# Another order of steps on every engine in a batch-pipelined transformer kernel

## The reference

```
L0: x  = LN(x  + MHA(x, ctx; 16 heads of 16, causal, length mask))    attention 0
    x  = LN(x  + MHA(x, ctx; 16 heads of 16, length mask))            attention 1
    x  = LN(x  + live * (fc2(relu(fc1(x)))))
L1: h  = x + Wo * GQA(rms(x), rms(ctx); 16 heads of 64, 4 kv heads, rope, additive mask)   attention 2
    x  = h + Wdown * (silu(Wgate rms(h)) * (Wup rms(h)))              width 1024
L2: x  = x + Wo * MHA(LN(x), LN(ctx); 16 heads of 16)                 attention 3
L3: x  = LN(x + Wo * MHA(x, ctx; 16 heads, scores * f(mask), clipped to +-50))             attention 4
```

## Time and profile before

| what | value |
|---|---|
| median of three runs | 4441.46 us |
| the profiled execution's own time | 4448.31 us |
| its span | 4446.5 us |
| granted TensorE clock, mean | 0.99 of full speed |
| busy: TensorE matmul / weight load | 92% / 78% of the span |
| busy: VectorE / ScalarE / GpSimd | 66% / 61% / 28% of the span |
| first store issued / 61st store issued | 246.99 us / 4283.08 us |

### The profile page before, as it was taken

One profiled execution on the slowest core, in us unless ns is written; L12 is line 12 of the kernel. 1 busy time (PEld: TensorE's weight loads), 2 busy tenths in 40 slices (PEclk: granted clock), 3 DMA queues, 4 the chain that ended last, 5 costly groups with the idle time before them and its releaser, 6 DMA issues.

```text
span 4446.5 us, 116614 instructions
## 1 busy us (share of the span) xinstructions
PE 4086.8 (92%) x45024; PEld 3473.5 (78%) x45024; DVE 2928.1 (66%) x7395; ACT 2694.5 (61%) x8513; POOL 1233.9 (28%) x2247
## 2 busy tenths in 40 slices
PE   4899999999999999999999999999999999999996
PEld 3778778787787787787787887787787877877875
DVE  2576676676666666766766766766766766766664
ACT  2566666656656656656656666666666666566563
POOL 0232322322322322323323323323223223223221
...
DMA packets 47341, 52.92 MB, mean 12 GB/s; under 512 B 5328, under 2 KB 46288, under 8 KB 46416
## 3 DMA queue, kind: packets, MB, share of 16 engines
...
## 4 chain that ended last, share of the span: by engine, by line
PE 42%; DVE 40%; issue 10%; POOL 5%; ACT 2%; DVEq 0%; DMA 0%; POOLq 0%; ACTq 0%
PE gen_ps L481 25%; PE gen_ps L473 9%; DVE negmax L957 4%; DVE masked L944 4%; POOL rstd L779 4%; DVE masked L951 4%; PE gen_ps L598 3%; DVE st L919 2%; DVE xs L929 2%; DVE zn L914 2%; ACT prob L724 2%; PE gen_ps L587 2%; PE scores_ps L556 2%; DVE negmax L946 2%; PE scores_ps L563 1%
## 5 line engine op out<-in xcount | busy, mean ns | idle before, releaser
L481 PE MATMUL gen_ps<-actT,w_sb 128*128 128x128 f32 x11264 | 1394.5, 277 | 3.4 <-ACT actT L694 3.3
L481 PEld LDWEIGHTS gen_ps<-actT,w_sb 128*128 128x128 f32 x11264 | 1325.8, 193 | 23.0 <-ACT actT L694 6.2
L724 ACT ACTIVATE prob<-scores_ps,negmax 128x128 f32<-128x128 f32 x3072 | 859.8, 406 | 330.6 <-DVE negmax L957 330.6
L779 POOL TENSOR_TENSOR rstd<-ve,consts 128x1 f32<-128x1 f32 x448 | 282.9, 631 | 1525.0 <-DVE ve L921 1000.0
L473 PE MATMUL gen_ps<-consts,prob 128*128 128x128 f32 x4096 | 591.0, 279 | 65.1 <-ACT prob L724 63.1
L694 ACT ACTIVATE probT<-gen_ps 128x512 f32<-128x512 f32 x1024 | 585.8, 638 | 59.7 <-PE gen_ps L473 59.7
L473 PEld LDWEIGHTS gen_ps<-consts,prob 128*128 128x128 f32 x4096 | 467.8, 142 | 184.9 <-ACT prob L724 147.2
L957 DVE TENSOR_REDUCE negmax<-scores_ps 128x4 f32<-128x512 f32 x768 | 492.0, 682 | 82.7 <-PE scores_ps L563 82.2
L481 PE MATMUL gen_ps<-w_sb,actT 128*128 128x256 f32 x2048 | 532.3, 383 | 2.7 <-ACT actT L694 1.9
L481 PE MATMUL gen_ps<-w_sb,wide 128*128 128x256 f32 x2048 | 467.9, 381 | 1.2 <-issue 1.2
L694 ACT ACTIVATE actT<-gen_ps 128x256 f32<-128x256 f32 (+1 forms) x576 | 276.5, 480 | 301.4 <-PE gen_ps L473 294.0
...
## 6 DMA issues: line engine op xcount, KB each, us to landing
ctx_rms<-x_dram SPq DMA_DIRECT2D x64, 128.0 KB, 2.2
ctx<-ctx_dram SPq DMA_DIRECT2D x64, 128.0 KB, 2.2
mask<-mask_dram SPq DMA_DIRECT2D x128, 64.0 KB, 2.0
out_dram<-res SPq DMA_DIRECT2D x64, 128.0 KB, 1.7
...
```

The lines of the kernel that those rows point to most:

```text
L481: last = nc.tensor.matmul(ps, lhsT(c), rhs(c), start=(c == 0), stop=(c == chunks - 1))
L724: ins = nc.scalar.activation(prob[:, N % 4, k, :], scores_ps[:, u, k * S:(k + 1) * S], ACT.Exp, bias=negmax[:, N % 4, k:k + 1])
L779: nc.gpsimd.tensor_tensor(dst, src, const("expo")[:, 0:width], ALU.pow)\
```

## The change

`PERIOD` goes from 66.01 to 67.32 and all times in `LIFE` are others. No step is added or removed, and no wait, buffer or instruction is altered; what changes is the order in which each of the four engines meets the steps. The core of the diff:

```diff
-PERIOD = 66.01
+PERIOD = 67.32
...
-    ("xT", 0, 0, {"PE": 0.00, "ACT": 2.67, "DVE": 14.33}),
-    ("queries", 0, 0, {"PE": 16.81, "DVE": 24.76}),
-    ("keys", 0, 0, {"PE": 17.38, "ACT": 22.00}),
...
+    ("xT", 0, 0, {"PE": 2.23, "ACT": 0.00, "DVE": 15.62}),
+    ("queries", 0, 0, {"PE": 8.34, "DVE": 18.60}),
+    ("keys", 0, 0, {"PE": 12.59, "ACT": 20.84}),
...
-    ("attended", 0, 0, {"PE": 49.73, "DVE": 52.29, "POOL": 44.45}),
-    ("q2", 2, 1, {"PE": 118.91, "DVE": 122.20, "POOL": 112.04}),
+    ("attended", 0, 0, {"PE": 60.47, "DVE": 70.60, "POOL": 66.81}),
+    ("q2", 2, 1, {"PE": 125.81, "DVE": 134.69, "POOL": 123.09}),
...
-    ("norm", 4, 0, {"DVE": 250.95}),
+    ("norm", 4, 0, {"DVE": 270.05}),
```

More of the change, by code:

```diff
@@ new lines @@
+    ("xT", 0, 0, {"PE": 2.23, "ACT": 0.00, "DVE": 15.62}),
+    ("queries", 0, 0, {"PE": 8.34, "DVE": 18.60}),
+    ("keys", 0, 0, {"PE": 12.59, "ACT": 20.84}),
+    ("first_row", 0, 0, {"PE": 28.83, "DVE": 35.23}),
+    ("scores", 0, 0, {"PE": 35.17}),
+    ("soft", 0, 0, {"ACT": 39.93, "DVE": 52.57}),
+    ("soft", 0, 1, {"ACT": 48.63, "DVE": 52.58}),
+    ("soft", 0, 2, {"ACT": 50.15, "DVE": 54.63}),
+    ("soft", 0, 3, {"ACT": 50.61, "DVE": 54.91}),
+    ("turn", 0, 0, {"PE": 50.81, "ACT": 51.92}),
@@ new lines @@
+    ("turn", 0, 1, {"PE": 50.83, "ACT": 53.93}),
+    ("turn", 0, 2, {"PE": 51.20, "ACT": 54.22}),
+    ("turn", 0, 3, {"PE": 52.20, "ACT": 54.53}),
+    ("values", 0, 0, {"PE": 59.02, "ACT": 59.88}),
+    ("attended", 0, 0, {"PE": 60.47, "DVE": 70.60, "POOL": 66.81}),
+    ("stats", 0, 0, {"DVE": 72.35, "POOL": 68.27}),
+    ("ctx_norms", 0, 0, {"DVE": 72.01, "POOL": 76.98}),
+    ("tr", 1, 0, {"PE": 72.31, "ACT": 72.06}),
+    ("norm", 0, 0, {"DVE": 76.79, "POOL": 73.71}),
+    ("queries", 1, 0, {"PE": 73.76, "DVE": 82.99}),
@@ new lines @@
+    ("keys", 1, 0, {"PE": 74.92, "ACT": 74.53}),
+    ("first_row", 1, 0, {"PE": 76.06, "DVE": 89.90}),
+    ("scores", 1, 0, {"PE": 83.79}),
+    ("soft", 1, 0, {"ACT": 89.90, "DVE": 90.57}),
+    ("soft", 1, 1, {"ACT": 91.02, "DVE": 92.87}),
+    ("turn", 1, 0, {"PE": 91.61, "ACT": 98.08}),
+    ("turn", 1, 1, {"PE": 93.97, "ACT": 98.66}),
+    ("soft", 1, 2, {"ACT": 97.90, "DVE": 95.09}),
+    ("turn", 1, 2, {"PE": 95.14, "ACT": 101.36}),
+    ("turn", 1, 3, {"PE": 96.98, "ACT": 102.02}),
+    ("values", 1, 0, {"PE": 97.61, "ACT": 102.27}),
@@ new lines @@
+    ("soft", 1, 3, {"ACT": 97.97, "DVE": 100.17}),
+    ("attended", 1, 0, {"PE": 99.83, "DVE": 110.20, "POOL": 102.65}),
+    ("x2T", 1, 0, {"PE": 102.91, "ACT": 105.93}),
+    ("h", 1, 0, {"PE": 105.25, "ACT": 109.16}),
+    ("z", 1, 0, {"PE": 106.66, "DVE": 123.12, "POOL": 109.83}),
+    ("stats", 1, 0, {"DVE": 116.20, "POOL": 107.35}),
+    ("mean_square", 2, 0, {"DVE": 124.66, "POOL": 111.85}),
+    ("norm_x3", 1, 0, {"ACT": 116.79, "DVE": 123.14}),
+    ("norm", 1, 0, {"DVE": 119.39}),
+    ("tr", 2, 0, {"PE": 120.38, "ACT": 125.10}),
@@ new lines @@
+    ("q2", 2, 1, {"PE": 125.81, "DVE": 134.69, "POOL": 123.09}),
+    ("q2", 2, 0, {"PE": 124.24, "DVE": 132.22}),
+    ("rms_norm", 2, 0, {"DVE": 125.81}),
+    ("kv2", 2, 0, {"PE": 127.74, "DVE": 137.21, "POOL": 131.56}),
+    ("scores", 2, 0, {"PE": 134.16}),
+    ("soft", 2, 0, {"ACT": 139.86, "DVE": 145.37}),
+    ("soft", 2, 1, {"ACT": 140.13, "DVE": 145.76}),
+    ("prob_norm", 2, 0, {"DVE": 154.41, "POOL": 145.41}),
+    ("soft", 2, 2, {"ACT": 149.54, "DVE": 147.97}),
+    ("turn", 2, 0, {"PE": 150.47, "ACT": 155.38}),
@@ new lines @@
+    ("soft", 2, 3, {"ACT": 151.13, "DVE": 150.69}),
+    ("turn", 2, 1, {"PE": 151.36, "ACT": 156.49}),
+    ("prob_norm", 2, 1, {"DVE": 154.58, "POOL": 156.79}),
+    ("turn", 2, 2, {"PE": 156.86, "ACT": 157.62}),
+    ("prob_norm", 2, 2, {"DVE": 157.55, "POOL": 156.97}),
+    ("turn", 2, 3, {"PE": 157.99, "ACT": 158.37}),
+    ("out2", 2, 0, {"PE": 158.68, "ACT": 159.54}),
+    ("out2", 2, 1, {"PE": 158.87, "ACT": 165.03}),
+    ("prob_norm", 2, 3, {"DVE": 161.13, "POOL": 163.02}),
+    ("o2", 2, 0, {"PE": 161.83, "ACT": 166.51, "DVE": 167.60}),
@@ new lines @@
+    ("nT", 3, 0, {"PE": 164.69, "ACT": 169.52}),
+    ("gate", 3, 0, {"PE": 166.58, "ACT": 170.54, "DVE": 181.48}),
+    ("mean_square", 3, 0, {"DVE": 169.45, "POOL": 166.60}),
+    ("up", 3, 0, {"PE": 167.92, "DVE": 186.98}),
+    ("rms_norm", 3, 0, {"DVE": 170.47}),
+    ("gate", 3, 1, {"PE": 171.47, "ACT": 175.80, "DVE": 187.54}),
+    ("up", 3, 1, {"PE": 173.98, "DVE": 189.66}),
+    ("down", 3, 0, {"PE": 182.99, "DVE": 192.29, "POOL": 181.59}),
+    ("tr", 3, 0, {"PE": 187.15, "ACT": 190.39}),
@@ new lines @@
+    ("queries", 3, 0, {"PE": 190.14, "DVE": 196.18}),
+    ("keys", 3, 0, {"PE": 190.95, "ACT": 193.00}),
+    ("scores", 3, 0, {"PE": 192.62}),
+    ("norm_x4", 3, 0, {"DVE": 194.47}),
+    ("soft", 3, 0, {"ACT": 194.50, "DVE": 199.82}),
+    ("soft", 3, 1, {"ACT": 195.52, "DVE": 199.99}),
+    ("turn", 3, 0, {"PE": 195.83, "ACT": 198.14}),
+    ("soft", 3, 2, {"ACT": 196.61, "DVE": 200.33}),
+    ("soft", 3, 3, {"ACT": 198.01, "DVE": 202.35}),
+    ("turn", 3, 1, {"PE": 198.18, "ACT": 199.36}),
@@ new lines @@
+    ("turn", 3, 2, {"PE": 198.55, "ACT": 200.92}),
+    ("turn", 3, 3, {"PE": 201.24, "ACT": 201.53}),
+    ("values", 3, 0, {"PE": 204.21, "ACT": 203.44}),
+    ("attended", 3, 0, {"PE": 207.70, "DVE": 213.90}),
+    ("zT", 3, 0, {"PE": 209.69, "ACT": 212.54}),
+    ("o", 3, 0, {"PE": 213.84, "DVE": 224.80, "POOL": 213.93}),
+    ("tr", 4, 0, {"PE": 215.51, "ACT": 221.83}),
+    ("queries", 4, 0, {"PE": 220.09, "DVE": 233.60}),
+    ("keys", 4, 0, {"PE": 224.24, "ACT": 226.49}),
+    ("mask4", 4, 0, {"PE": 230.46, "DVE": 236.07}),
@@ new lines @@
+    ("scores", 4, 0, {"PE": 231.67}),
+    ("soft", 4, 0, {"ACT": 237.12, "DVE": 240.83}),
+    ("soft", 4, 1, {"ACT": 237.33, "DVE": 240.94}),
+    ("soft", 4, 2, {"ACT": 239.66, "DVE": 241.38}),
+    ("soft", 4, 3, {"ACT": 241.63, "DVE": 243.42}),
+    ("values", 4, 0, {"PE": 244.82, "ACT": 245.03}),
+    ("attended", 4, 0, {"PE": 252.25, "DVE": 260.12}),
+    ("o", 4, 0, {"PE": 256.55, "DVE": 263.46, "POOL": 252.67}),
+    ("zT", 4, 0, {"PE": 253.62, "ACT": 256.43}),
+    ("norm", 4, 0, {"DVE": 270.05}),
```

## The result

The changed kernel takes 4509.15 us (median of 4 runs, 4505.61 to 4512.69) against 4442.45 before: ratio 1.015, 95% interval 1.0133 to 1.0168, that is 1.5% slower. The forecast was 4453 us and the range ended at 4500.

The account below looks back on a forecast made before the run. TensorE and VectorE taking turns bound the kernel. Period 23.4 + 42.3 + 1.65 = 67.4 us against 67.27, times 60 is +8 us, plus some 4: 4460 as profiled, median 4453 us; range 4375 to 4500.

Parts of the forecast that it names:

- the layout of one period: One period of the new lists laid by hand with the old trace's durations: 67.4 us against 67.27.
- VectorE's part: From the read-out of q2.0 to that of o3, VectorE leads without an idle place: 23.4 us.
- TensorE's 43.8 for 43.95: From tr4 to the end of q2.0, TensorE leads: 42.3 us packed plus 1.65 of stops.
- The hold by GpSimd: norm4's L926 and L929 on VectorE wait for GpSimd's L817 and L819 after q2.1: 1.58 us a period.
- rival 1: GpSimd doesn't hold VectorE at norm4: period 65.8 us, time 4358, or 4406 with half of it; chance 0.22.
- Rival 2: GpSimd holds more of VectorE's run (L911, L901, L897 to L899, L926): likely 0.8 us a period, 4501 us; chance 0.2.
- Fill and drain: Start and end of the kernel: later first output, drain shorter by as much; 0, with 8 us to each side.
- Rivals 3 and 4: 3: load into norm4's slot late, 60 us per us beyond, chance 0.05; 4: TensorE's stops all return, 4441 us, chance 0.13.

Follow-up runs that it names:

- e5: Changed kernel with the tie broken (z on TensorE from 106.66 to 106.68) and the transposes of turn3.1 made four times over: 4470.57 us, 1.0065.
- e3: Changed kernel with the tie broken (up.1 always first) and norm4 on VectorE moved just ahead of q2.1's read-out: 4411.19 us, 0.9934.
- e11: Changed kernel with its tie left as it is and the transposes of turn3.1 made four times over: 4486.38 us, 1.0096.
- e2: Changed kernel with TensorE's time of z from 106.66 to 106.64, so z precedes up.1 in all 63 periods: 4546.18 us, 1.0236.
- e8: e7 with rms_norm3 put ahead of first_row0 on VectorE: 4371.32 us, 0.9837.
- e4: e3 with norm4 still further ahead on VectorE, before the read-out of q2.0: 4390.07 us, 0.988.
- e7: e4 with o3's read-out ahead of first_row1 and the zero-row test xT0 behind it on VectorE: 4324.37 us, 0.9731.

## Why the prediction was wrong

- **What bounds the kernel, and the layout of one period: right.** Of the stops laid out, the trace has nT 0.34 (0.36 forecast), x2T 0.40 (0.57), zT4 0.35 (0.42), turn3.2 1.31 (1.5), turn3.3 0.40 (0.4), tr1 0.42 (0.65), queries1 0.25 (0.3), tr4 1.08 (0.8), tr3 0.06 (0.30), and those before zT3 and behind the exponentials are gone. VectorE's run is not without an idle place, as the prediction had it: it waits 0.51 us for GpSimd's reciprocal square root at norm0, as it did before (the sum carries this inside its 12.15 us), and 0.21 ahead of the last soft2. The undisturbed period is 67.6 us, forecast 67.4: VectorE's part 23.8 for 23.4, TensorE's 43.8 for 43.95. e5, which has neither tie nor slow clock, takes 28 us more than the 4442.45 of before (30 more than the 4440.5 of its own group); the forecast had 12.
- **The hold by GpSimd: right in place and size**, so rival 1 is out. L926 and L929 at 1.18 and 1.39 us against "about 1.2 and 1.4". e3 moves norm4 out of it and gains 59 us; with that one step moved and the tie broken, the new order beats the old one by 29 (4411.19 against 4440.5). What is won without it was over-stated: 1.6 us less on VectorE brought 1.0, for the two reasons given at e3. One reading beside it was wrong: the prediction says that only instructions of 0.73 us and less are seen as holders in its rows, and its own row of L787 has 0.90.
- **Rival 2, more of VectorE's run held: true in part.** L911 in attended0 went from 0.23 to 0.37, L901 in first_row1 from 0.34 to 0.55 us. That is 0.35 us a period, nearly all of the 0.4 by which VectorE's part was missed, and that part is over the 23.6 us from which on the prediction let rival 2 decide. I had given it 0.2 as a chance and left it out of the sum. The Trainium skill, VectorE: DVE Perf Modes, section "Mode 2×_2P — use both read ports for one tensor", counts tensor_scalar from SBUF, which both are, among the operations that can use both ports. That these two run in such a mode was not shown, and no run gave them a place without GpSimd in the new order.
- **The list that the sum walks: wrong in 14 periods.** The prediction laid out one list for all periods. Two steps had the same phase, and rounding set their order; where z comes first, it waits 0.72 us for the ReLU of h, a stop that the sum doesn't have. Shown by e11 against e5: 16 us.
- **The clock: missing.** TensorE's clock was taken as full in the whole steady state, as in the trace of before. The step that failed is the one that put stops in new places and counted each at its own length: with turn3.2's 1.3 us, followed by 0.4 at turn3.3 just ahead of scores2, the granted clock is at half there in 21 of 50 periods, at some 0.8 us each. Shown by e11 against the changed kernel: 23 us. The kernel before also stopped for 0.52 and 0.38 us ahead of scores2, and for 1.17 before zT3, and kept its clock. With the first stop filled the clock doesn't fall (e5), so the stop is needed, but it is not all of it: in e2 the clock fell in only 8 periods. In e8 a single stop of 1.56 us a period, at x2T, left it at full; the one stretch at half clock there follows a stop of 1.92 us.
- **Fill and drain: within its bound.** +5 us, forecast 0 with 8 to each side.
- **Rivals 3 and 4: not seen.** TensorE waited for a load of x once, for 5.9 us at the start, as in the kernel before. And stops don't come back in full wherever they are moved: e3, e4 and e7 each removed some and gained.

So of the 67 us measured, order and hold make 28 (before to e5), the tie 16 (e5 to e11) and the clock 23 (e11 to the changed kernel). These are three steps of one chain, so that they add up proves nothing; what each is worth rests on the run that ends it. The forecast of 4453 us was 56 too low: 16 in the part that it had laid out, and 16 and 23 in two terms that it didn't have.
